# Building the inverse routing beside the last attention scores, and adding the experts' rows with VectorE and TensorE together

## What is computed

```python
x = x + 0.5 * ffn(layernorm(x))        # base linear + 8 experts of rank 8, top 2 by a router
x = x + attention(layernorm(x))        # 16 heads of 16
x = x + 0.5 * ffn(layernorm(x))
x = x + 0.5 * moe(layernorm(x))        # 32 experts, 4 given choices per token
x = x + latent_attention(layernorm(x))
x = x + 0.5 * moe(layernorm(x))

def moe(h):                            # topk_idx, topk_weight: [2048, 4]
    for every token n and choice k: e = topk_idx[n, k]
        y[n] += topk_weight[n, k] * down[e] @ (silu(gate[e] @ h[n]) * (up[e] @ h[n]))
```

## Time and profile before

| what | us |
|---|---|
| median of 3 runs | 1489.26 (1489.18 to 1489.72) |
| the profiled execution, own time | 1499.06 |
| its span, first to last instruction | 1497.0 |
| TensorE busy | 1267.1 (85%) |
| VectorE busy | 950.7 (64%) |
| ScalarE busy | 671.1 (45%) |
| GpSimd busy | 502.9 (34%) |

### The profile page before, as it was taken

One profiled execution on the slowest core, in us unless ns is written; L12 is line 12 of the kernel. 1 busy time (PEld: TensorE's weight loads), 2 busy tenths in 40 slices (PEclk: granted clock), 3 DMA queues, 4 the chain that ended last, 5 costly groups with the idle time before them and its releaser, 6 DMA issues.

```text
span 1497.0 us, 22302 instructions
## 1 busy us (share of the span) xinstructions
PE 1267.1 (85%) x6633; PEld 816.1 (55%) x6634; DVE 950.7 (64%) x2721; ACT 671.1 (45%) x1706; POOL 502.9 (34%) x495
## 2 busy tenths in 40 slices
PE   6769898898888599998778889889889997899980
PEld 4514243343336578887545455556546556788870
DVE  6786758777756622224498978887897793123227
ACT  2205655555672055553245444453554461255540
POOL 2054040052315645552111211351152153355550
PEclk7959998999999699999999999999999998899995
DMA  7527543073304166554011100020010112344538
GB/s 283 108 25 117 179 85 42 1 150 147 151 19 162 72 231 203 181 166 152 3 54 29 29 1 1 11 103 1 7 36 15 57 43 102 102 157 156 164 124 280
DMA packets 78687, 147.91 MB, mean 99 GB/s; under 512 B 11693, under 2 KB 60014, under 8 KB 75758
## 3 DMA queue, kind: packets, MB, share of 16 engines
q1 hardware_dynamic: 62782, 104.36, 24.8%
q0 software_dynamic: 15360, 41.96, 7.8%
q10 hardware_dynamic: 432, 0.17, 0.0%
HBM read 83.15 MB, written 62.91 MB: 98 GB/s over the span
## 4 chain that ended last, share of the span: by engine, by line
PE 54%; DVE 27%; issue 7%; ACT 6%; POOL 3%; DMA 2%; another core or an unknown queue 0%; SPq 0%; DVEq 0%; POOLq 0%; ACTq 0%
PE m_psG L1164 12%; PE m_psY L1180 5%; DVE a_t L1599 4%; DVE a_mx L852 4%; PE a_psO L456 3%; PE m_psX L1155 3%; DVE a_nb L1607 3%; PE a_psA L1358 3%; PE a_psU L431 3%; PE a_psU L1340 3%; PE a_psW L397 2%; ACT a_pr L1469 2%; POOL rows_dram L166 2%; PE a_psS L442 2%; DVE x L1134 2%
## 5 line engine op out<-in xcount | busy, mean ns | idle before, releaser
L166 POOL DMA_INDIRECT outs_dram<-m_ys,dest x192 | 184.5, 961 | 162.8 <-ACT m_ys L1099 129.8
L1469 ACT ACTIVATE a_pr<-a_psA,a_nb 128x512 f32<-128x512 f32 (+3 forms) x256 | 132.8, 525 | 218.5 <-DVE a_nb L1607 218.0
L1119 DVE TENSOR_TENSOR m_hm<-m_psG,m_sg 128x128 f32<-128x128 f32 x192 | 56.0, 292 | 266.5 <-ACT m_sg L1093 159.2
L852 DVE TENSOR_REDUCE a_mx<-a_psU 128x1 f32<-128x512 f32 x256 | 163.7, 684 | 67.4 <-PE a_psU L431 65.5
L1164 PE MATMUL m_psG<-arena,m_xgT 128*128 x768 | 202.2, 386 | 2.2 <-ACT m_xgT L1087 1.6
L1525 POOL TENSOR_TENSOR a_q<-a_q,a_t 64x512 f32<-64x512 f32 x64 | 80.8, 1263 | 353.3 <-DVEq L1602 329.4
L166 POOL DMA_INDIRECT rows_dram<-a_xd,slot x128 | 139.3, 1089 | 165.3 <-DVE a_xd L146 78.4
L587 ACT ACTIVATE a_P<-a_psS 128x512 f32<-128x512 f32 x256 | 142.7, 597 | 50.8 <-PE a_psS L442 44.7
L1164 PEld LDWEIGHTS m_psG<-arena,m_xgT 128*128 128x128 f32 x768 | 130.6, 190 | 19.0 <-issue 7.1
L1607 DVE TENSOR_REDUCE a_nb<-a_psA 128x1 f32<-128x512 f32 (+3 forms) x256 | 113.3, 485 | 34.9 <-PE a_psA L1360 24.3
L431 PE MATMUL a_psU<-arena 96*128 96x512 bf16 x256 | 106.7, 419 | 32.8 <-DVE a_mx L852 30.7
(11 more groups left out here) (270 smaller groups left out, 2319.2 us busy)
## 6 DMA issues: line engine op xcount, KB each, us to landing
m_xg<-rows_dram SPq DMA_DIRECT2D x46, 512.0 KB
arena<-in_mo_w SPq DMA_DIRECT2D x9, 2048.0 KB
arena<-part_dram SPq DMA_DIRECT2D x96, 128.0 KB
arena<-outs_dram SPq DMA_DIRECT2D x16, 512.0 KB, 3.9
rows_dram<-a_P SPq DMA_DIRECT2D x6, 1024.0 KB, 14.1
part_dram<-a_part SPq DMA_DIRECT2D x16, 384.0 KB, 5.3
rows_dram<-arena SPq DMA_DIRECT2D x6, 1024.0 KB, 15.5
m_xg<-outs_dram SPq DMA_DIRECT2D x8, 512.0 KB, 4.6
```

Of the source, the lines that this page charges most:

```text
L166: pool.indirect_dma_start(out=rows_dram, out_offset=bass.IndirectOffsetOnAxis(ap=slot[:, c:c + 1], axis=0), in_=row, in_offset=None).then_ ...
L852: dve.tensor_reduce(mx[g % 2][:, 4 * kt + qt:4 * kt + qt + 1], psU[n % 2][:, :], AX, ALU.max).then_inc(u_free, 1)
L1469: ins = act.activation(pr[S % 2][:, AT[t]:AT[t] + (t + 1) * P], psA[:, AT[t]:AT[t] + (t + 1) * P], ACT.Exp, bias=nb[S % 2][:, t:t + 1], sc ...
```

## The change

**Inverse routing.** The one-hots are cut into smaller instructions (four `low` of 128 x 512, four `block` of 128 x 384 a quarter; two sets of four `tensor_scalar` in place of one `tensor_tensor` and one `tensor_scalar`) and put at other points: quarters 0 and 1 at points 2 to 5, 7, 10 to 13 and 15 of i = 4, quarter 2 at `OP` and before the last `GM`, quarter 3 half there and half before the last `LA`. TensorE multiplies quarters 0 and 1 before the last feed-forward's transposes, quarter 2 before its `TH`, quarter 3 at the end; 23 and 11 of the 30 and 13 idle products go. `dest` numbers rows 256 + 512 t + 4 p + k now.

**Last rows by halves.** `last_rows(c)` does addition, statistics, scales and normalised rows for tiles 2c and 2c + 1, and writes into `fxn` in place of `xd`.

**The sum at the end.** Token 4 p + j of a sequence sits in partition p as tile j, so that x has to be rearranged: it is stored to `x_dram` in four transfers during the blocks and loaded back in the new layout in four more. 40 diagonal matrices of half the weights are made on VectorE, one every other block. After the blocks all rows are loaded by 8 transfers into the arena of the expert weights (8 MB in all, none waits for a buffer); TensorE adds two choices of even tiles and three of odd ones in PSUM, VectorE adds the other 24 and the PSUM sum. Stores are three of four tiles, then two, one and one.

```diff
-            IDLE_LAST = {("ao", B - 1, 0): 3, ("ao", B - 1, 1): 3, ("x", 2, B - 1, 0): 30, ("h", 2, B - 1): 13}
+            IDLE_LAST = {("ao", B - 1, 0): 3, ("ao", B - 1, 1): 3, ("x", 2, B - 1, 0): 7, ("h", 2, B - 1): 2}
+            INVERT_AT = {("x", 2, B - 1, 0): (0, 1), ("h", 2, B - 1): (2,)}
...
+    ONES_AT = {p: (q, (n,)) for q, at in ((0, (2, 3, 4, 5)), (1, (10, 11, 12, 13))) for n, p in enumerate(at)}
+    ONES_AT[OP] = (2, (0, 1, 2, 3))
+    VALUES_AT = {7: 0, 15: 1}
...
+            def last_rows(c):
+                b, two = B - 1, slice(2 * c, 2 * c + 2)
+                add(("l", 2, b, c), b, c)
+                released(dve, ("l", 2, b, c))
+                for j in (2 * c, 2 * c + 1):
+                    t = b * TPB + j
+                    ins = dve.bn_stats(r.stats[:, 6 * t:6 * t + 6], x[:, t * D:(t + 1) * D])
...
+                inverse_root(dve, link, sd.var[:, two], sd.rstd[:, two], sd.tmp[:, two])
+                for j in (2 * c, 2 * c + 1):
+                    t = b * TPB + j
+                    dve.tensor_scalar(fxn[:, j * D:(j + 1) * D], x[:, t * D:(t + 1) * D], sd.mv[:, 2 * j:2 * j + 1],
+                                      sd.rstd[:, j:j + 1], ALU.subtract, ALU.mult).then_inc(xd_ready, 1)
...
-            high_ones(1)
-            for q in range(2, QUARTERS):
-                low_ones(q)
-                high_ones(q)
             invert()
...
+        LOADS = [(0, 1), (1, 2), (2, 4), (4, 6), (6, 8), (8, 12), (12, 14), (14, 16)]
+        SAVES = [(u, u + 4) for u in range(0, TILES - 4, 4)] + [(TILES - 4, TILES - 2), (TILES - 2, TILES - 1), (TILES - 1, TILES)]
+        MIXED = [range(u * TOPK, u * TOPK + 2 + u % 2) for u in range(TILES)]
+        PARK_AT, BACK_AT = (4, 6, 8, 10), (12, 14, 16, 18)
...
+                    dve.tensor_scalar(diag[:, n * P:(n + 1) * P], ident[:, :], by_four[:, c:c + 1], None, ALU.mult).then_inc(diag_ready, 1)
...
+                    for c in range(u * TOPK, (u + 1) * TOPK):
+                        if c not in d_index:
+                            link(dve.scalar_tensor_tensor(out=xu, in0=pk[:, c * D:(c + 1) * D], scalar=by_four[:, c:c + 1], in1=xu,
+                                                          op0=ALU.mult, op1=ALU.add))
+                    dve.wait_ge(mixed, u + 1)
+                    dve.tensor_tensor(xu, banks[u % len(banks)][:, 0:D], xu, ALU.add).then_inc(added, 1)
...
+                stay_warm(pe, psX[0], ident, 28)
...
+                    for c in MIXED[u]:
+                        n = d_index[c]
+                        ins = pe.matmul(banks[u % len(banks)][:, 0:D], diag[:, n * P:(n + 1) * P], pk[:, c * D:(c + 1) * D],
+                                        start=(c == MIXED[u][0]), stop=(c == MIXED[u][-1]))
```

More of the change, by code:

```diff
@@ L795, in side @@
                     gates_end(*ffn_at(i, p, GB))
+                if ffn_at(i, p, LA) == (2, B - 1):
+                    all_ones(3, (2, 3))
+                    block_values(3)
+                    for c in range(2):
+                        last_rows(c)
+                    return
                 if ffn_at(i, p, LA):
@@ L1033, in moe_stage @@
         saved = [sem(f"saved{i}") for i in range(NY)]
-        picked = [sem(f"picked{i}") for i in range(NP)]
+        if result is not None:
+            out, written, by_four, by_four_src, x_dram = result
+            picked = [sem(f"picked{i}") for i in range(len(LOADS))]
+            added, mixed, diag_ready, weights_four = (sem(n) for n in ("added", "mixed", "diag_ready", "weights_four"))
+            parked, back = sem("parked"), sem("back")
+            diag = sb("diag", [P, sum(map(len, MIXED)) * P])
+            d_index = {c: n for n, c in enumerate(c for cs in MIXED for c in cs)}
+            pk = weights[:, 0:NC * D]
+            of_four = lambda b: out[b].rearrange("(p j) d -> p (j d)", j=TPB)
         @block.sync
@@ L1806, in program @@
         moe = lambda tag, placed, stored, loads, latent, result: moe_stage(
-            nc, block, sem, tag, r, ident, arena[:, :], (experts_in, 16 * loads), slot, weight, block_expert, rows_dram, placed, stored,
+            nc, block, sem, tag, r, ident, arena[:, :], (experts_in, 16 * loads), block_expert, rows_dram, placed, stored,
             outs_dram, dest, dest_in, latent, result)
```

201 lines of the change are left out of this document (136 added, 65 removed).

## The result

The changed kernel is faster, by less than forecast. Timed beside one another, its median was 1482.95 us against 1491.17 of the kernel before: a ratio of 0.9947 (95% interval 0.9929 to 0.9964), 8.2 us. Two further comparisons, on two different chips, gave 1485.15 against 1494.28 (0.994, 0.992 to 0.996) and 1486.45 against 1494.79 (0.9943, 0.9922 to 0.9964). The forecast was 14.5 us and 1474.8. The time of 1482.95 lies in the range of 1467 to 1485, but the size of the change does not hold: 8.2 to 9.1 us, some 0.55%, where 14.5 was forecast. The kernel before was itself 1.9 to 5.5 us above the 1489.26 that the forecast started from.

A forecast was written before the change was run, and what follows sets the result against it. No single engine bounds the kernel: GpSimd's scatters end the first layer, TensorE bounds the expert stages, VectorE the final sum. 9.3 - 2.3 + 7.5 = 14.5 us takes 1489.26 to 1474.8, range 1467 to 1485.

The forecast's parts named there:

- Part 1: One-hots cut and placed beside the last scores: mostly hidden in VectorE's waits, low-rank product 1.0 us late.
- The 3.8 us before `LA`: Last half quarter of one-hots and the values on VectorE before `LA`: 3.8 us, hidden in a wait of 5.03.
- Part 2: Last rows by halves: first scatter 2.0 us earlier, 16 scatters 20.0 us instead of 27.3, end 9.3 us earlier.
- the 2.0 for the earlier first scatter: Last batch's first scatter at 491.0 in place of 493.01, 2.0 us earlier.
- Part 3: First expert stage starts cold after TensorE idles from about 505 to 514.5; half clock costs 2.3 us.
- Part 4: Parked x and diagonals in the second expert stage's blocks: hidden, cost 0.
- Cost 0: Charge for moving 4 MB of x out and back and making 40 diagonals during the second stage's blocks: nothing.
- The rival: Parking holds up the second stage's block loads, eight times 1.5 us, 12 in all: 1486.8; chance 0.05.
- Part 5: Last sum shared by VectorE and TensorE, one wait before tile 8: end at 1489.5 instead of 1497.0, 7.5 us earlier.
- The dip of the clock: Wait before tile 8 puts TensorE at half clock, 2 us lost; chance 0.18 together with slow stores.
- The sum of terms: Whole kernel: 9.3 - 2.3 + 7.5 = 14.5 us faster, median from 1489.26 to 1474.8.

The follow-up runs named there:

- r_before: The kernel before, unchanged, traced a second time for its stages; span of that trace 1490.3 us.
- e_warm: 54 idle products ahead of the first expert stage in place of 36, against the changed kernel; 1484.1 us, ratio 0.9941 to the kernel before.

## Why the prediction was right and wrong

- **Part 1, one-hots beside the last scores: right for the scores, wrong before `LA`.** The charge was 1.0 us; the changed kernel's first gate row came 1.0 us late in the first profiles, and the way from the batch before to it took 0.8 to 1.9 us more than in before. The cut quarters fit into the waits there. The 3.8 us before `LA` were called hidden by a wait of 5.03; in r_before, at full clock, the wait is 2.83, and they are not.
- **Part 2, the scatters: right in mechanism, the step into it too high.** 7.3 us by the missing one-hots, as worked out. The term that was mis-sized is the 2.0 for the earlier first scatter: it measured 0.5 on average (gate row 1.3 later, the way from it to the scatter 1.8 shorter in place of 3.0). It rested on one trace, the slowest of four here: the low-rank product took 3.75 us at half clock, where the four show 1.97, 3.0, 3.4 and 3.75, and the copy ahead of it was 1.2 us late. On average the first layer gains 7.9, not 9.3. I had read the clock of other rows and not of this one.
- **Part 3, the cold start: right in place, a little high.** The stage began at a clock of 0.50 and was back at 1.00 by 520, and the stretch was 1.5 us longer, charged 2.3. The reason was in part another: I had TensorE idle from 505 on; its products in fact trickled until 513.
- **Part 4, parking: wrong, and the largest miss.** The step that failed is "Cost 0", with its reason that "the first expert stage carries extra weight loads in the same way". Those are loads into SBUF; the parked x goes out, and beside each of the four transfers out (in e_warm beside three) a read of the expert number took 1.4 to 1.5 us in place of about 0.4, and TensorE stood for 0.8 to 0.9. Measured 3.5 us in the stage; without parking it is gone (176.5), and without the read the stalls are (174.4). The rival named the right part, with the wrong mechanism (a late block load) and a price of 12.
- **Part 5, the sum: right.** 7.4 against 7.5, with the long wait where it was placed. The loads ran at full rate, 419 GB/s from 1460 to 1478 us. The Trainium skill ("DMA: Bandwidth & Descriptors", Specifications) gives 358 GB/s as a core's limit at the HBM; by that, as an estimate, the end would have been 3.5 us longer, and the trace does not agree. The dip of the clock, a rival of 2 us, came in four of fourteen traces with the new end and cost 1.5 to 2.5 us.
- **The sum of terms** was made against one profile, and its starting level against three times. That the time fell into the range was luck in part: the range was drawn for 14.5 us less than 1489.26, and a smaller gain met a higher start. -9.3 by the means of stages in place of -14.5 is 3.5 (parking) + 1.4 (the earlier first scatter) + 0.9 (latent stage, chance) - 0.8 (cold start) + 0.1.

## What to carry to other kernels

Before a bulk transfer is put beside a stage at the limit of TensorE, list what the engines' sequencers (the parts that run the instruction streams) read there, not only what the matmuls read. Here the read of a number in SBUF on which an address hangs took up to 1.1 us more beside a store of 512 KB from SBUF to DRAM, and it stood in no list of waits. Take the granted clock of each row that carries a term of the sum, and a second trace, before its duration is used as a price. Where TensorE is kept busy beside a long row of scatters, try few wide products in place of many small ones: here they left no gap, and the gain was 1 us at most.

## What the runs showed of the hardware

- TensorE's read of one number from SBUF took 0.30 to 0.76 us in a second expert stage without parked x, up to 1.04 us beside a transfer out of 256 KB and 1.36 to 1.52 us beside one of 512 KB (23 of 24 reads; the other took 0.76). In three traces a single read of the first expert stage took 0.9 to 1.1 us.
- Beside long rows of scatters, a queue of small idle products ran some 60 passes at 0.15 us and then one to three in 1.3 us, the spacing of the scatters (GpSimd's own rows: 0.96 + 0.30). 36 passes of 512 columns had no gap, nor had 72 small ones of which most ran after the last scatter. That instructions are supplied slowly meanwhile is inferred, not shown.
- The first scatter beside `tensor_tensor` work took longer by just that work (2.92 = 0.96 + 1.96; in before 2.71 = 0.96 + 1.75). Later ones lost less, 0.08 to 0.40 us beside short comparisons and 0.40 to 1.59 in before.
- In the two traces compared, the clock falls at the same places of the program by different amounts. The same latent stage took 586.9 to 594.3 us; the time of the changed kernel spread over 12.5 us (1477.8 to 1490.3).
